# Attention and routed FFN on one core: batch 0's score units ahead of the later projections, and GpSimd's constants in a later place

## The reference

```
x = x + attention(layernorm(x), context)     # 16 heads of 16, causal
x = x + ffn(layernorm(x))                    # 16 experts, top 4, plus a shared expert
attention: q = xn @ Wq.T; k, v = split(ctx @ Wkv.T); softmax(causal(q k.T / 4)) v @ Wout.T
```

## Time and profile before

| | |
|---|---|
| median of three runs | 204.12 us (203.25 to 207.0) |
| the profiled execution | 206.07 us, span of its instructions 204.3 us |
| busy: PE / DVE / POOL / ACT | 183.2 / 127.8 / 97.5 / 80.0 us |
| DMA | 28.94 MB, mean 142 GB/s |

### The profile page before, as it was taken

The page is one execution under the profiler, slowest core; times in us unless marked ns, Lnnn a source line. Parts: engine busy times, 40 slices in busy tenths (PEclk is TensorE's granted clock), DMA queues, the critical chain, the costliest instruction groups (busy, mean ns, idle before and its releaser), DMA issues.

```text
span 204.3 us, 3906 instructions
## 1 busy us (share of the span) xinstructions
PE 183.2 (90%) x1362; PEld 137.0 (67%) x1362; DVE 127.8 (63%) x360; ACT 80.0 (39%) x173; POOL 97.5 (48%) x129
## 2 busy tenths in 40 slices
PE   7887988989897999899989997998999999999980
PEld 2665645766574777578846684796878877677860
DVE  2584589697769457993484746878675554353054
ACT  3565722656266425651278412512133322432000
POOL 7816998577345102730054100033588888777002
PEclk9999999999999999999999999999999999999999
DMA  6769999993199969730861066955135444554776
GB/s 169 181 133 130 129 125 132 131 129 65 56 262 299 137 115 275 241 103 5 267 214 51 3 189 208 282 168 173 55 77 73 61 89 88 77 77 53 185 253 205
DMA packets 22459, 28.94 MB, mean 142 GB/s; under 512 B 2457, under 2 KB 17801, under 8 KB 22441
## 3 DMA queue, kind: packets, MB, share of 16 engines
q1 hardware_dynamic: 18944, 23.06, 51.6%
q0 software_dynamic: 3184, 5.38, 13.5%
q10 hardware_dynamic: 313, 0.27, 0.5%
HBM read 15.91 MB, written 6.42 MB: 109 GB/s over the span
## 4 chain that ended last, share of the span: by engine, by line
PE 31%; DMA 12%; POOL 7%; issue 7%; DVE 6%; ACT 1%; DVEq 1%; POOLq 0%; ACTq 0%
DMA odd_d<-y_rows,tok_i 9%; PE s_ps L1495 9%; PE m_ps L1511 4%; DMA xn_t<-odd_d 3%; PE m_ps L1453 3%; PE o_ps L1415 3%; POOL out L636 2%; POOL q_parts L624 2%; PE m_ps L1571 2%; POOL odd_d L636 2%; DVE top L926 2%; PE m_ps L1477 2%; PE t_ps L1399 2%; PE m_ps L1430 1%; POOL k_parts L624 1%
## 5 line engine op out<-in xcount | busy, mean ns | idle before, releaser
L561 POOL TENSOR_SCALAR_AFFINE_SELECT probs<-probs 128x256 f32<-128x256 f32 (+1 forms) x48 | 23.2, 486 | 42.1 <-ACT probs L702 40.8
L926 DVE TENSOR_REDUCE top<-s_ps 128x2 f32<-128x512 f32 (+1 forms) x48 | 32.1, 686 | 5.5 <-PE s_ps L1365 4.9
L702 ACT ACTIVATE probs<-t_ps 128x512 f32<-128x512 f32 x48 | 27.6, 597 | 8.3 <-PE t_ps L1399 6.0
L1495 PE MATMUL s_ps<-xn_t,sgu 128*128 128x256 f32 (+1 forms) x96 | 23.5, 384 | 0.7 <-DVE s_mid L1011 0.7
L1399 PE MATMUL t_ps<-q_rows,k_rows 128*128 128x256 bf16 (+1 forms) x128 | 19.6, 247 | 1.9 <-ACT probs L702 1.1
L1495 PEld LDWEIGHTS s_ps<-xn_t,sgu 128*128 128x128 f32 (+1 forms) x96 | 16.5, 182 | 3.9 <-DVE s_mid L1011 1.1
L1362 PE MATMUL s_ps<-mask_b,ident_b 128*128 128x256 bf16 (+1 forms) x48 | 15.0, 312 | 4.0 <-DVE top L926 3.6
L1365 PE MATMUL s_ps<-k_rows,q_rows 128*128 128x128 bf16 (+1 forms) x128 | 18.4, 246 | 0.0
L624 POOL DMA_INDIRECT xn<-xn_d,tok_i x4 | 3.9, 980 | 24.4 <-DVE tok_i L1104 23.8
L1399 PEld LDWEIGHTS t_ps<-q_rows,k_rows 128*128 128x128 bf16 x128 | 10.1, 98 | 6.4 <-ACT probs L702 2.9
L766 ACT ACTIVATE xg_t<-t_ps 128x256 f32<-128x256 f32 x16 | 6.1, 384 | 20.3 <-PE t_ps L1589 19.5
(11 more groups left out here) (191 smaller groups left out, 392.0 us busy)
## 6 DMA issues: line engine op xcount, KB each, us to landing
k_rows<-k_parts SPq DMA_DIRECT2D x24, 128.0 KB, 8.2
q_rows<-q_parts SPq DMA_DIRECT2D x24, 128.0 KB, 8.9
k_rows<-in_w_dn SPq DMA_DIRECT2D x12, 176.0 KB
out<-xs SPq DMA_DIRECT2D x8, 256.0 KB, 2.2
wgu_early<-in_w_gu SPq DMA_DIRECT2D x4, 352.0 KB
q_rows<-in_w_gu SPq DMA_DIRECT2D x4, 352.0 KB
v_ones<-in_w_gu SPq DMA_DIRECT2D x4, 352.0 KB
probs<-in_w_gu SPq DMA_DIRECT2D x4, 352.0 KB
```

The costliest lines, as they stand in the source:

```text
L561: nc.gpsimd.affine_select(out=v, in_=v, compare_op=ALU.is_ge, fill=0.0, base=0, pattern=[[0, v.shape[1]], [1, P]], channel_multiplier=-1). ...
L702: t_ring.emptied(nc.scalar.activation(probs[:, g % 2, u, :], t_ring.bank(job)[:], ACT.Exp, scale=HD ** -0.5), job)
L926: s_ring.emptied(nc.vector.tensor_reduce(dst, src, AX.X, ALU.max), job)
L1495: last = nc.tensor.matmul(s_ring.bank(("gu", b, c))[0:size, S * half:S * half + S], sgu[:, hc, half, at:at + size], xn2_t[:, hc, S * b:S * ...
```

## The change

Batch 0's score units come right behind k2 on TensorE, and x2, q2, v2, x3 and v3 stand between them, one after each of the units 1, 3, 5, 7 and 9. Before, x2, q2, x3 and v2 stood ahead of them. The idle products before k0 become 11 instead of 9. ScalarE's order follows (k2's lead part now comes before x2's copy), and its square root for batch 3 comes before q1's copy. VectorE splits q1 one step earlier and k2 one step later: after the maxima of unit 0. GpSimd makes the low part of k2 before both fills, and does the fifteen routing constants between the second and the third DMA of zeros, with unchanged instructions. The slots of the rows stay as they are.

```
-KEEP_BUSY = {("k", 0): 9, ("q", 0): 3, ("x", 1): 2, ("s", 0, 0): 4}
+KEEP_BUSY = {("k", 0): 11, ("q", 0): 3, ("x", 1): 2, ("s", 0, 0): 4}
...
+OPENING_FILL = {1: (("x", 2),), 3: (("q", 2),), 5: (("v", 2),), 7: (("x", 3),), 9: (("v", 3),)}
...
-    steps.extend([("k", 0), ("x", 0), ("q", 0), ("k", 1), ("v", 0), ("x", 1), ("q", 1), ("v", 1),
-                  ("k", 2), ("x", 2), ("q", 2), ("x", 3), ("v", 2)])
+    steps.extend([("k", 0), ("x", 0), ("q", 0), ("k", 1), ("v", 0), ("x", 1), ("q", 1), ("v", 1), ("k", 2)])
     for u in range(3 * NG):
         steps.append(("s", 0, u))
-        if u == 4:
-            steps.append(("v", 3))
+        steps.extend(OPENING_FILL.get(u, ()))
...
             last_part("q", 1)
+            last_part("k", 2)
             pad_rows(q_rows, 1, ROW_BUFS, 0.0)
-            last_part("k", 2)
             pad_rows(k_rows, 1, ROW_BUFS, ONE_PAIR)
             constant(nc.gpsimd.memset(zero_rows[:], 0.0))
...
+            def late_constants():
...
                         pool.dma_start(out[T:T + CAP], zero_rows[:]).then_inc(zeros_stored, 16)
+                        late_constants()

                         pool.wait_ge(shift_in[1], 16)
...
             normalise(2)
+            std_of(3)
             copy_q(1)
             copy_v(1)
-            std_of(3)
+            copy_k(2)
             copy_x(2)
             normalise(3)
-            copy_k(2)
+            copy_q(2)
+            copy_v(2)
             copy_x(3)
-            copy_v(2)
-            copy_q(2)
             copy_v(3)
...
+            split(1, 1, "q")
             scale_of(3)
-            split(1, 1, "q")
-            split(2, 0, "k")
             for u in range(NS):
                 maxima(0, u)
+                if u == 0:
+                    split(2, 0, "k")
```

More of the change, by code:

```diff
@@ L567, in _ @@
             last_part("q", 1)
+            last_part("k", 2)
             pad_rows(q_rows, 1, ROW_BUFS, 0.0)
-            last_part("k", 2)
             pad_rows(k_rows, 1, ROW_BUFS, ONE_PAIR)
             constant(nc.gpsimd.memset(zero_rows[:], 0.0))
[L573 to L594, removed]
+            def late_constants():
+                link(nc.gpsimd.memset(cst[:], 1.0))
+                link(nc.gpsimd.affine_select(out=cst[:], in_=cst[:], compare_op=ALU.is_gt, fill=0.0,
+                                             base=0, pattern=[[1, P]], channel_multiplier=-1))
+                link(nc.gpsimd.tensor_copy(above_b[:], cst[:]))
+                link(nc.gpsimd.iota(cst[:], pattern=[[1, P]], base=1, channel_multiplier=0,
+                                    allow_small_or_imprecise_dtypes=True))
+                link(nc.gpsimd.tensor_copy(slot_iota[:], cst[:].unsqueeze(2).to_broadcast([P, CAP, NT])))
+                link(nc.gpsimd.iota(spare_row[:], pattern=[[0, 1]], base=T, channel_multiplier=1,
+                                    allow_small_or_imprecise_dtypes=True))
+                link(nc.gpsimd.iota(minus_slot[:], pattern=[[0, 1]], base=0, channel_multiplier=-1,
+                                    allow_small_or_imprecise_dtypes=True))
+                link(nc.gpsimd.iota(cst[:], pattern=[[0, P]], base=0, channel_multiplier=1,
+                                    allow_small_or_imprecise_dtypes=True))
+                v = cst[:].rearrange("p (t e) -> p t e", t=NT)
+                link(nc.gpsimd.tensor_copy(tok_vals[:, :, :, 0], v))
+                link(nc.gpsimd.iota(v, pattern=[[P, NT], [0, E]], base=-T, channel_multiplier=0,
+                                    allow_small_or_imprecise_dtypes=True))
+                link(nc.gpsimd.tensor_copy(tok_vals[:, :, :, 1], v))
+                link(nc.gpsimd.memset(cst[:], 1.0))
+                link(nc.gpsimd.tensor_copy(tok_vals[:, :, :, 2], v))
+                link(nc.gpsimd.memset(key[:], MARK))
+                constant(nc.gpsimd.memset(four[:], MARK))
```

## The result

The changed kernel takes 205.78 us (median of 12 runs, 204.68 to 207.26), the kernel before 204.12 us (median of 12 runs beside them, 203.03 to 207.0). The ratio is 1.0084 with a 95% interval of 1.005 to 1.0119: slower by 1.7 us, under the 2% band but clear of its own interval. I had forecast 204.1, no change. The profiled execution took 207.26 us, its span is 205.5. Some executions of most kernels are over 1.5% slower than the kernel's fastest; the ratios leave them out and the medians don't (they are three of order_only's six), and the profiles of order_only and b_busy come from such executions.

A forecast was written before the change was run, and what follows sets the result against it. TensorE, busy for 90% of the span, was taken as the bound, batch 1's start hanging on its chain and the row-copy landing. Terms 0.85 + 0 - 0.85 + 0.1 = +0.1 on 204.12, said as 204.1 us; range 202.2 to 207.0.

The forecast's parts named there:

- What bounds the start of batch 1: End of the opening: two paths with equal ends, row-copy landing at 36.9 and TensorE's chain at 36.57 us.
- the queue is backed up: SyncE's row copies: batch 1's last copy takes 12.0 us to land because the DMA engines are busy throughout.
- by just as much as q0: Sign to look for: the landing of batch 1's last row copy moves by the same amount as q0.
- Part 1: TensorE's opening: score units start 1.5 us earlier, batch 1 starts 0.85 us later.
- The walk: Stepping through both programs with profiled durations from batch 0's first unit; put batch 1's first unit at 37.95 us.
- Part 2: VectorE's cast of k2: 0.43 us instead of 2.04 with no GpSimd fill beside it; cost 0.
- Part 3: Two more idle products before k0: clock rises earlier, 0.85 us faster, ends 0.1 slower and 1.35 faster.
- Rival B: TensorE's clock falls back in the new gap from 19.3 to 23.4: 1.9 us slower, 206.0; chance 0.17.
- Part 4: GpSimd's constants moved: TensorE stalls 0.6 us at batch 1's first output product, mostly given back, cost 0.1.
- Rival C: The stall by GpSimd's constants isn't given back: +0.9 us, 205.0; chance 0.08.

The follow-up runs named there:

- order_only: Changed kernel with 9 idle products before k0 and GpSimd's constants at their old place, behind the fills; 208.35 us (six runs) against 203.97, ratio 1.0122.
- b_busy: Kernel before with four idle products between k2 and x2 and three ahead of q2; 203.71 us against 204.62, ratio 0.9978.
- hybrid2: Changed kernel with x2, q2 back ahead of the units, k2's split ahead of all maxima, 9 idle products before k0, constants early; 204.6 us, ratio 1.0007.
- b_extra_rows: Kernel before with two more row copies in SyncE's queue among those of batch 1; 206.16 us against 204.6, ratio 1.0072.
- a_warm20: Changed kernel with 20 instead of 4 idle products ahead of batch 0's first score unit; 205.02 us, ratio 1.006 against the kernel before.
- b_k0_11: Kernel before with 11 instead of 9 idle products ahead of k0, nothing else; 204.24 us against 203.97, ratio 1.0004.
- b_late_consts: Kernel before with GpSimd's fifteen routing constants between its second and third DMA of zeros, nothing else; 204.39 us, ratio 1.0018.

## Why the prediction was wrong

**What bounds the start of batch 1: right, and tested.** Two paths with nearly equal ends, landing and chain. hybrid2 shortens one by 1.0 and gets 0.15, b_extra_rows lengthens the other and pays 1.8 of 1.9. My reason for the landing, "the queue is backed up", was right only for row copies: a copy to HBM passes beside them. Nor did the landing move "by just as much as q0": in the changed kernel it came 1.2 us earlier behind q0.

**Part 1, the order: right in mechanism and size.** Predicted +0.85, found 0.86 (U1 of a_warm20 against before, with the clock held). The walk had 14.5 us from the first unit to batch 1's first unit, a_warm20 has 14.42. The first unit was put 1.5 us earlier, it is 1.4; the wait of VectorE behind q2 was put at 1.4, it is 1.42; the idle stretch at 4.1, it is 4.12.

**Part 2, the cast: right.** 0.43, and the fills had enough cover. What I missed is that GpSimd's later fills leave no free place for its constants, so that the two edits hang together: in the new order early constants make batch 1's start 0.5 to 0.6 later.

**Part 3, the two idle products: the step that failed.** The prediction said "I take 0.85, above the middle". What was found is 0: in the profile after, k0 and x0 run at the lower clock as before, and q0 starts 3.78 us behind k0 as against 3.77; b_k0_11's ratio is 1.0004, and its interval ends at a gain of 0.7. Here I took a gain from a row that shows a single execution. The other profiles show that it isn't a property of the gap: with 9 products the distance from k0 to q0 was 3.77, 2.27, 3.95, 2.28, 2.65, 3.39 and 2.28 us, with 11 products 3.78, 2.53, 2.36, 2.28 and 2.66. Both clock levels occur with either number. Nor does the length of the gap decide: hybrid2's k0 had one of the two longest, 2.44 us, and its four products took 1.10 us, where the kernel before's took 2.04 behind 0.68.

```profile
7.59 1.10 PE L1311 MATMUL m_ps<-lat,wkv 128*128 128x256 f32 x4 [2.44 <-DMA wkv<-in_wkv_t]
```

What sets the level there stays open.

**Rival B, the clock in the gap: it happened, in the profile and, by their mean clocks of 0.977 to 0.991, most likely in all twelve runs.** I had given it 0.17, with a price of 1.9. Its price was 0.42 (a_warm20 against after, at U1): the mean of 0.94 from 27.2 to 30.0 puts its return near 27.5, within what the walk gave for a short low stretch (0.45). No row of before had a gap of over 1.1 us, so the trace couldn't tell, and there the warning of the Trainium skill (TensorE: Matmul & The Clock Gate, Why this matters for your kernels) against idle gaps in mid-kernel should have weighed more than the missing row; the row of after agrees with it (4.12 us of gap, granted clock 0.50 behind it). A second step that failed is this chance, not the mechanism; the price was too high, since the clock came back before q2.

**Part 4, the constants: the sign was right, the cover counted right, the give-back wrong.** Predicted a stall of 0.6 and "I take 0.1, ends 0 and 0.9"; found a stall of 0.40 and 0.45 at the rank product (b_late_consts). That is the third step that failed. Rival C, with its chance of 0.08, had the mechanism, and at 0.9 twice the price. A stall of TensorE was taken as absorbed because TensorE waits for VectorE later, but TensorE's two waits for VectorE stayed at 0.6 and 0.5 us; by the programs' order VectorE's work is itself queued behind TensorE's units.

**The sum.** 0.86 + 0 + 0.45 + 0.42 = 1.73, where 1.72 stand in the marks and 1.7 in the runs. The forecast had 0.85 + 0 - 0.85 + 0.1. The difference of 1.6 is the credit for the two idle products (0.85), the fall of the clock (0.42) and what the constants cost beyond the 0.1 (0.35). The range of 202.2 to 207.0 holds 205.78, the direction was not forecast.

## What to carry to other kernels

Work that is moved into another engine's waits must leave no idle stretch where it was: here the same products fitted into a wait ahead of a landing and lengthened the chain behind it. Don't count a stall on the leading engine as given back when what it later waits for depends itself on the stalled instructions. And before crediting a change with an effect on the start, look at how far the start moves from run to run; marks counted from a common instruction tell terms of 0.1 us apart where whole runs spread by 3 us.

## What the runs showed of the hardware

- The clock's level at the start of a program varies between executions of like kernels: from k0's start to q0's it takes 2.3 to 4.0 us, and k0, which waits for its weights, starts at 5.5 to 7.7 us. A gap of 2.44 us ahead of k0 left it at the higher level, one of 0.68 didn't.
- TensorE's clock fell to half in an idle stretch of 4.1 us behind four idle products, and was back within 3 us of work. It also fell in a stretch with waits of 1.01 and 0.69 us around four transposes (b_k0_11), which in the kernel before's own profile had left it full. Seven idle products in those waits cost nothing.
- 128 KB from SBUF to HBM in the same queue, between the row copies, did not delay batch 1's last landing (163 against 131 GB/s at the same busy share), while two further row copies of 128 KB delayed it by 1.9 us.
- Batch 1's last row copy landed 26.1 us behind q0's start in the changed kernel, against 27.3 before. In the twelve profiles it is that early only in the two (after and order_only) in which a transfer of 16 KB in the queue "instruction" came behind it (at 26.7 us, elsewhere at 20.7 to 21.9); that the one causes the other isn't shown. It no longer mattered there, since TensorE's chain ended later.
- A VectorE subtraction of 128x32 took 1.08 us beside a GpSimd cast of 1.04 us and 0.19 without one, and TensorE waited 0.5 us for it.
